# A sum made straight from PSUM behind a second transpose, and the normalisations of tokens moved from VectorE to GpSimd

## The reference

```python
x = x + _layernorm(_L0_attn_ref(_layernorm(x), ...))   # 16 heads of 64, latent width 64 for q and for k, v; rope; out + residual
x = x + _layernorm(_L0_ffn_ref(_layernorm(x), ...))    # router softmax, top 2 of 8 experts, hidden width 256, SiLU gate
```

## Time and profile before

| | us |
|---|---|
| median of 3 runs | 1662.54 (1661.48 to 1665.63) |
| the profiled execution, its own time | 1663.62 |
| its span | 1661.8 |
| PE busy (matmuls) | 1404.3, 85% |
| DVE busy | 1212.5, 73% |
| ACT busy | 1107.1, 67% |
| POOL busy | 1231.9, 74% |

### The profile page before, as it was taken

How to read it: one execution, slowest core, us unless ns; L and a number is a source line. 1 busy time by engine, 2 the same in 40 slices (tenths; PEclk the granted TensorE clock), 3 DMA queues, 4 the chain that set the end, 5 groups by cost and what they waited for, 6 DMA issues and landing times. The chain is left out here.

```text
span 1661.8 us, 45240 instructions
## 1 busy us (share of the span) xinstructions
PE 1404.3 (85%) x17718; PEld 904.0 (54%) x17718; DVE 1212.5 (73%) x2719; ACT 1107.1 (67%) x2136; POOL 1231.9 (74%) x749
## 2 busy tenths in 40 slices
PE   4899989998988989989988899999888887777630
PEld 1366656665545656656645556665455555566530
DVE  7788777777878788787777887777778875555353
ACT  2777767776667767767766677777666666355462
POOL 5588977986767678896766788987667788535574
PEclk7899999999999999999999999999999998789775
DMA  6333423422322223222321232322212421222332
GB/s 179 92 109 115 119 79 107 120 78 65 84 69 79 72 66 102 72 72 71 84 71 49 58 92 77 85 79 71 65 45 70 156 65 41 91 79 85 104 104 64
DMA packets 111232, 140.87 MB, mean 85 GB/s; under 512 B 17712, under 2 KB 59952, under 8 KB 110640
## 3 DMA queue, kind: packets, MB, share of 16 engines
q1 hardware_dynamic: 106928, 129.60, 27.9%
q0 software_dynamic: 4096, 8.40, 1.7%
HBM read 23.50 MB, written 19.92 MB: 26 GB/s over the span
## 5 line engine op out<-in xcount | busy, mean ns | idle before, releaser
L1844 POOL TENSOR_TENSOR probs_lo<-probs 128x1024 f16<-128x1024 f32 x312 | 655.8, 2109 | 233.2 <-ACT probs L1116 231.9
L1116 ACT ACTIVATE probs<-psum 128x512 f32<-128x512 f32 x1024 | 614.6, 602 | 228.3 <-PE psum L846 227.8
L1415 DVE CUSTOM_DVE_ANT_0 scan_out<-psum,ahead 128x512 f16<-128x512 f32 x512 | 349.0, 687 | 249.5 <-PE psum L744 223.8
L865 PE MATMUL psum<-cv,probs 128*128 128x66 f16 x4096 | 488.6, 195 | 23.7 <-POOL probs_lo L1844 23.7
L867 PE MATMUL psum<-cv,probs 128*128 128x64 f16 x4096 | 487.6, 196 | 0.0
L869 PE MATMUL psum<-cv,probs_lo 128*128 128x66 f16 x4096 | 486.2, 194 | 0.0
L867 PEld LDWEIGHTS psum<-cv,probs 128*128 128x128 bf16 x4096 | 388.1, 99 | 116.6 <-issue 13.2
L865 PEld LDWEIGHTS psum<-cv,probs 128*128 128x128 bf16 x4096 | 392.5, 99 | 87.5 <-POOL probs_lo L1844 20.4
L846 PE MATMUL psum<-q_max,k_ones 65*128 65x512 f16 x1024 | 401.8, 392 | 0.0
L844 PE MATMUL psum<-q_both,k_twice 128*128 128x512 f16 x1024 | 399.7, 390 | 0.0
L869 PEld LDWEIGHTS psum<-cv,probs_lo 128*128 128x128 f16 x4096 | 387.1, 100 | 0.0
(11 more groups left out here) (208 smaller groups left out, 1976.9 us busy)
## 6 DMA issues: line engine op xcount, KB each, us to landing
t_swapped<-t_sin SPq DMA_DIRECT2D x248, 128.0 KB, 2.1
k_twice<-qk_hi SPq DMA_DIRECT2D x128, 128.0 KB, 2.4
q_lone<-qk_hi SPq DMA_DIRECT2D x64, 128.0 KB, 2.4
q_both<-qk_hi SPq DMA_DIRECT2D x64, 128.0 KB, 2.3
q_both<-qk_lo SPq DMA_DIRECT2D x64, 128.0 KB, 2.4
q_max<-qk_hi SPq DMA_DIRECT2D x64, 128.0 KB, 2.4
k_ones<-qk_lo SPq DMA_DIRECT2D x64, 128.0 KB, 2.4
z_unit<-slots_in SPq DMA_DIRECT2D x46, 128.0 KB, 2.3
```

Source lines behind the costliest of these rows:

```text
L865: pe.matmul(acc, high[:, q * P:(q + 1) * P, 1], v[:, 0:VLO], start=opens, stop=False, skip_group_check=True)
L1116: act.activation(probs[s % 4][:, i, :], score_ps[tile % SCORE_BANKS], ACT.Exp, scale=SCALE).then_inc(probs_done, 1)
L1415: dve.tensor_tensor_reduce(scan_out[m % 2][:], bank[BANK_OF["base", n, m]], ahead[m % 2][:], 1.0, LOWEST, ALU.add, ALU.max, max_all[a][:, ...
L1844: pool.tensor_tensor(probs_lo[s % 4][:].rearrange("p a n -> p (a n)"), p, p.bitcast(BF16).rearrange("p (n two) -> p n two", two=2)[:, :, 1 ...
```

## The change

- `add_tokens` no longer reads `res_sb`. PE turns the same tokens of `oacc` a second time, in new jobs "again" at (2, 8) and (2, 10), and DVE makes `x_sb = x_sb * res_scale + psum`. That is the old sum times the token's deviation; `res_scale` is that deviation plus the inverse deviation of x. The four instructions for each half now read one operand from SBUF and one from PSUM.
- As the next norm does not see the token's scale but for its epsilon, its variance becomes `ln_var` (one more instruction on 128x8) with the bias `eps_twice`. `add_output` gives the scale back: four instructions of 128x128 for each half in place of one of 128x512.
- `normalise_batch` and `normalise_input` go to POOL. Each half is two instructions of 128x512, a subtraction and a multiplication with the token's numbers broadcast over the channels, at steps 3, 5, 7 and 9 of the pair, behind `rope_add`. For batch 3 all four stand together at unit 11, behind `low_hidden(11)`.
- Some statistics, means, deviations and inverses move by one step; ACT's two table changes go from step 15 to step 0 of the next pair.
- `route` compares the indices as they are, without the cast (line 1553).

```diff
-STAT0_AT, MEANS0_AT, DEV0_AT, INV0_AT = ((1, 12), (1, 13)), (1, 14), (1, 15), (2, 1)
-ADD_AT = ((2, 8), (2, 10))
-STAT1_AT, MEANS1_AT, DEV1_AT, INV1_AT = ((2, 12), (2, 13)), (2, 14), (2, 15), (3, 1)
-NORM_AT = ((3, 8), (3, 10))
+STAT0_AT, MEANS0_AT, DEV0_AT, INV0_AT = ((1, 12), (1, 14)), (1, 15), (2, 0), (2, 2)
+AGAIN_TURNS = ((2, 8), (2, 10))
+STAT1_AT, MEANS1_AT, DEV1_AT, INV1_AT = ((2, 12), (2, 14)), (2, 15), (3, 0), (3, 2)
+NORM_AT = ((3, 3), (3, 5), (3, 7), (3, 9))
...
-    return {("norm", 0): (k, 8), ("norm", 1): (k, 10), ("x", 0): (k, 11), ("x", 1): (k, 12),
+    return {("norm", 0): (k, 3), ("norm", 1): (k, 5), ("norm", 2): (k, 7), ("norm", 3): (k, 9), ("x", 0): (k, 11), ("x", 1): (k, 12),
...
+            if at == AGAIN_TURNS[half]:
+                jobs.append((1, ("again", epoch - 1, half)))
...
-PE_TOKENS, PE_INPUT, PE_LOGITS, PE_RANK = 3, 13, 15, 22
+PE_TOKENS, PE_AGAIN, PE_INPUT, PE_LOGITS, PE_RANK = 3, 7, 13, 15, 22
+POOL_NORM = 11
...
+                elif kind == "again":
+                    pe.wait_ge(x1_done, CHUNKS * n + (at + 1))
...
-                last.then_inc(mv_done[k], 1)
+                last.then_inc(mv_done[k] if k != 1 else mv1_parts, 1)
+                if k == 1:
+                    dve.wait_ge(mv1_parts, n + 1)
+                    dve.scalar_tensor_tensor(out=ln_var[:], in0=mv_of(0, n)[:, :, 1], scalar=LN_EPS, in1=mv_of(1, n)[:, :, 1],
+                                             op0=ALU.mult, op1=ALU.add).then_inc(mv_done[k], 1)
...
+            def residual_scale(n):
+
+                dve.wait_ge(dev_done[0], n + 1)
+                dve.tensor_tensor(res_scale[:], ln_dev[0][:], rstd_x[:, n * TILES:(n + 1) * TILES], ALU.add).then_inc(res_scaled, 1)
+
             def add_tokens(n, half):
-                dve.wait_ge(inv_done[0], n + 1)
+                dve.wait_ge(res_scaled, n + 1)
+                dve.wait_ge(o_turned, 2 * CHUNKS * n + CHUNKS + (half + 1))
+                src = job_bank("again", n, half)
                 for t in tile_range(half):
-                    last = dve.scalar_tensor_tensor(out=x_sb[:, t, :], in0=res_sb[:, t, :], scalar=inv_of(0, n)[:, t:t + 1],
-                                                    in1=x_sb[:, t, :], op0=ALU.mult, op1=ALU.add)
+                    last = dve.scalar_tensor_tensor(
+                        out=x_sb[:, t, :], in0=x_sb[:, t, :], scalar=res_scale[:, t:t + 1],
+                        in1=src[:, t % HALF_TILES * P:(t % HALF_TILES + 1) * P], op0=ALU.mult, op1=ALU.add)
                 last.then_inc(x1_done, 1)
-
-            def normalise_input(n, half):
-                dve.wait_ge(inv_done[1], n + 1)
-                for t in tile_range(half):
-                    last = dve.tensor_scalar(z_sb[:, t, :], x_sb[:, t, :], mv_of(1, n)[:, t, 0:1], inv_of(1, n)[:, t:t + 1],
-                                             ALU.subtract, ALU.mult)
-                last.then_inc(z_done, 1)
...
-                dve.tensor_tensor(x1_all[n][:, tiles, :], x1_all[n][:, tiles, :], y_got[n][:, 0, tiles, :], ALU.add).then_inc(result_done, 1)
+                for t in tile_range(half):
+                    last = dve.scalar_tensor_tensor(out=x1_all[n][:, t, :], in0=x1_all[n][:, t, :], scalar=inv_of(0, n)[:, t:t + 1],
+                                                    in1=y_got[n][:, 0, t, :], op0=ALU.mult, op1=ALU.add)
+                last.then_inc(result_done, 1)
...
+            def normalise_batch(b, half, part):
...
+                if part == 0:
+                    if b == 1:
+                        pool.wait_ge(ln_y_inverse, 4)
+                    else:
+                        pool.wait_ge(x_next, 16 * (b - 1))
+                    pool.tensor_tensor(rows, rows, over_rows(moments_x[:, at, 0]), ALU.subtract).then_inc(n_centred, 1)
+                else:
+                    pool.wait_ge(n_centred, CHUNKS * (b - 1) + (half + 1))
+                    pool.tensor_tensor(rows, rows, over_rows(rstd_y[:, at]), ALU.mult).then_inc(n_ready, 1)
+
+            def normalise_input(n, half, part):
...
+                if part == 0:
+                    pool.wait_ge(inv_done[1], n + 1)
+                    pool.tensor_tensor(rows, x_sb[:, tiles, :], over_rows(mv_of(1, n)[:, tiles, 0]), ALU.subtract).then_inc(z_centred, 1)
+                else:
+                    pool.wait_ge(z_centred, CHUNKS * n + (half + 1))
+                    pool.tensor_tensor(rows, rows, over_rows(inv_of(1, n)[:, tiles]), ALU.mult).then_inc(z_done, 1)
```

More of the change, by code:

```diff
@@ L1656, in beside @@
                     for half in range(CHUNKS):
-                        if (r, s) == when["norm", half]:
-                            normalise_batch(b, half)
                         if (r, s) == when["latent", half]:
@@ L1735, in beside_unit @@
                     inverses(1, EARLY)
-                    for half in range(CHUNKS):
-                        normalise_input(EARLY, half)
                 for part in ROUTE_PARTS:
@@ L1938, in _ @@
                 low_hidden(unit)
+                if unit == POOL_NORM:
+                    for half in range(CHUNKS):
+                        for part in range(2):
+                            normalise_input(EARLY, half, part)
                 if unit in SEND_UNITS:
```

66 lines of the change are left out of this document (40 added, 26 removed).

## The result

The changed kernel takes 1593.43 us (median of 4 runs, 1590.84 to 1596.16) against 1662.24 us (4 runs, 1661.48 to 1665.63) for the kernel before on the same chip. The ratio is 0.9582 [0.9561, 0.9604]: 68.8 us or 4.2% less. The profiled execution has a span of 1594.4 us and a mean TensorE clock of 0.947 (before 1661.8 and 0.927).

A forecast was written before the change was run, and what follows sets the result against it. It took PE as the bound, at 37.5 us per undisturbed pair, with nine pairs slowed by waits for DVE and a low clock. Terms -72 + 7 + 12 + 2 + 3 + 1.4 = -46.6 gave 1616 us, range 1597 to 1642.

The forecast's parts named there:

- term 6: Moving means, deviations and inverses by one step leaves the cost of ACT's table changes as it was: 0, up to 3 us either way.
- the cast: Removing the cast in `route` gains 0, as the pairs' waits stay with the comparisons behind it.
- the expert stage and the end: Unit 11's gain and loss cancel, transposes at unit 7 cost 1 us, the last half 0.4: +1.4 us.
- Term 3: The "again" jobs, PE turns and DVE adds in three pairs, cost 7 us, between 0 and 15.8.
- terms 4 and 7: POOL's added norm instructions in six pairs cost 12 us; z and x turns meeting POOL's later results cost 3 us.
- term 5: Six small DVE instructions with two SBUF operands, `residual_scale` and `ln_var`, may wait for POOL: 2 us, 0 to 12.
- terms 1 and 2: In the nine pairs, PE's waits for DVE (45.3 us) and the low clock behind them (27 us) go: together 72 us.
- costs nothing: Rival: POOL's added norm instructions fit in its 5.3 us of idle time per pair; 1601 us, chance 0.2.
- POOL takes DVE's place: Rival: POOL's work overruns PE's pace, six pairs keep their length, only the `add_tokens` pairs gain; 1647 us, chance 0.14.

The follow-up runs named there:

- Experiment 1: Kernel before with only the second transposes, the sum from PSUM and the token-scale work; norms, steps and cast as before: 1638.79 us, ratio 0.9846.
- experiment 2: Kernel before with only the norms moved to POOL as broadcast instructions: 1626.59 us, ratio 0.9797.
- Experiment 5: Changed kernel with each of the 24 broadcast norm instructions inside pairs done a second time on POOL into a spare tile: 1609.06 us, ratio 0.9692.
- experiment 6: Changed kernel with the norms back on DVE as rows of four 128x128 instructions, at steps 3 and 7: 1624.91 us, ratio 0.9789.
- experiment 10: Changed kernel with its broadcast norm instructions issued by DVE in place of POOL, at the same steps: 1648.17 us, ratio 0.9673.
- experiment 3: Kernel before with only the steps of statistics, means, deviations and inverses moved: 1658.46 us, ratio 0.9968.
- experiment 7: Changed kernel with statistics, means, deviations and inverses put back at their old steps: 1597.69 us, ratio 0.9619.
- Experiment 4: Kernel before with only the cast in the routing left out: 1659.1 us, ratio 0.998.
- experiment 12: The changed kernel repeated word for word on another chip, against the kernel before: 1592.07 us, ratio 0.9582.
- experiment 11: Changed kernel with only ranks, places and low rows moved to earlier steps of their pair: 1597.31 us, ratio 0.961.
- experiment 8: Changed kernel with only the norm of batch 3, at unit 11, back on DVE: 1594.29 us, ratio 0.9622.
- experiment 9: Changed kernel with routing, ranks, places and low rows moved to earlier steps of the same pairs: 1639.1 us, ratio 0.9629.

## Why the prediction was right in kind and low in size

**What bounds the kernel: right.** PE stood behind DVE in the nine pairs, and its clock was at 0.90 to 0.96 in them. With the stalls gone the nine pairs lost 58.1 us at equal cuts (48 predicted), and PEclk is 1.00 in eight of them.

**Which steps failed.** Two. First, the terms that were put at nothing or given the wrong sign: the moved steps (term 6) measured 5.3 us and the cast 3.3 by themselves, and the expert stage and the end took 4.4 us less and not 1.4 more. Second, the price of what was added in the nine pairs: terms 3, 4, 5 and 7 took back 24 us of the 72, some 10 too much. By their windows the sum from PSUM alone gained 21.4 us where my terms leave 17, and the norms alone 36.7 where they leave 31. Each is taken up below. Beside that, two readings of the rows were wrong.

**The removed waits and clock, terms 1 and 2 (-72): right within some 4 us.** Experiment 1 takes 21.4 us out of the three `add_tokens` pairs, where my sum for them was 26.2 - 7 - 2 = 17. The missing 4 us lie in these three terms together. The small instructions of term 5 or the "again" jobs cost less, or the removal was more; no run separates them. Term 3 itself can be read in the "tokens" pairs, which hold the same work: they take 118.3 us after, 5.9 over the three undisturbed pairs of the earlier trace rows, against 7 taken. Its upper end was wrong: of the 15.8 us that the earlier trace rows has over the earlier trace rows, 7.4 were the late cut.

**POOL's load, terms 4 and 7 (+15): too dear.** The waits and the clock of the six pairs were 46.1 us in my terms, and experiment 2 gained 36.7 there, so 9.4 were given back. Not all of that is POOL's: I had counted the waits for `max_turned` as gone whole, and 7.2 us of them are left in the six pairs after (1.2 in each). Whether POOL's load keeps them there isn't shown. Two more errors met. The form costs 1.04 us alone, not 1.27, but nearly 2 among DVE's work, which is outside the 1.2 to 1.4 that I expected; and I take it, from PE's short waits, that part of this was covered; no run shows it. Experiment 5 prices a further four at 2.9 us a pair, above my 2, which I put down to the last cover being gone. The rival "costs nothing" is refuted by it. The rival "POOL takes DVE's place" is refuted by experiment 2: the six pairs are 36.7 us shorter though POOL is busy 96% of them. DVE's `low` did get longer as expected, a mean of 1640 ns (before 1541 by the group of line 1436), and PE has no wait over 0.15 us for it in the nine pairs:

```profile
L1442 DVE TENSOR_TENSOR probs_lo<-probs 128x1024 f16<-128x1024 f32 x200 | 327.9, 1640 | 4.3 <-ACT probs L1129 4.0
```

**Why the norms were dear: only partly understood.** I took the meeting with POOL's long instructions at steps 8 and 10 as the cause, and wrote that each of the small instructions waits for one of POOL's. The timeline of DVE shows less than that. Before, one of the two rows of four in such a pair was held long and the other ran free (first two lines, here 1.10 us at step 8 and 6.43 at step 10). In experiment 6 both are held once (2.50 us), and in experiment 10 the single instructions take 1.2 to 1.6 us each (last two lines):

```profile
1216.47 1.10 DVE L1503 TENSOR_SCALAR res_sb<-x_sb,ln_mv,ln_inv 128x128 f32<-128x128 f32 x4
1221.63 6.43 DVE L1503 TENSOR_SCALAR res_sb<-x_sb,ln_mv,ln_inv 128x128 f32<-128x128 f32 x4
```
```profile
1165.87 2.50 DVE L1531 TENSOR_SCALAR res_sb<-x_sb,ln_mv,ln_inv 128x128 f32<-128x128 f32 x4
1178.01 2.50 DVE L1531 TENSOR_SCALAR res_sb<-x_sb,ln_mv,ln_inv 128x128 f32<-128x128 f32 x4
```
```profile
1163.56 1.23 DVE L1406 TENSOR_TENSOR res_sb<-x_sb,ln_mv 128x512 f32<-128x512 f32 x1
1168.34 1.56 DVE L1409 TENSOR_TENSOR res_sb<-res_sb,ln_inv 128x512 f32<-128x512 f32 x1
```

The two rows of experiment 6 hold DVE for 5.0 us of a pair, the four instructions of experiment 10 for 5.2 here; so it isn't their sum that makes the 21.4 us, but where and in how long pieces it falls. That a long piece holds back the scan behind it is shown by PE's waits for `max_turned` and `max_all`; how much is the length of a piece and how much its step is argued, not shown. The timeline of POOL after shows the same meeting from the other side; its norms take 1.9 to 2.0 us there, and PE's waits in that pair (shown above) hold none for POOL:

```profile
1148.36 1.91 POOL L1891 TENSOR_TENSOR res_sb<-x_sb,ln_mv 128x512 f32<-128x512 f32 x1 [0.99 <-DVE ln_inv L1497]
1150.23 1.89 POOL L1852 TENSOR_TENSOR probs_lo<-probs 128x1024 f16<-128x1024 f32 x1
1152.09 1.27 POOL L1836 TENSOR_TENSOR rot<-rot,t_swapped 128x512 f32<-128x512 f32 x1
1153.33 2.02 POOL L1894 TENSOR_TENSOR res_sb<-res_sb,ln_inv 128x512 f32<-128x512 f32 x1
```

By the Trainium skill, "SBUF — State Buffer", section Who interferes with whom, a VectorE instruction with two SBUF inputs or in a two-port mode and one of GpSimd that reads SBUF hold each other out of a shared port pair for whole instructions; these figures agree (1.04 us alone, 1.91 and 2.02 beside DVE). The Trainium skill's rule in "GPSIMD Engine Reference", section 4.1 Engine selection, that elementwise work belongs on VectorE, pointed the wrong way here: by experiments 6 and 10 both forms on DVE were slower than the broadcast one on POOL, by 29.0 and 7.6 us for six pairs. The prediction set 2.5 us of POOL, in two instructions, against 1.1 of DVE for its factor of two; the nearer pair of like instructions in its rows is 1.27 us and 0.69.

**The moved steps, term 6 (0, up to 3 either way): failed.** They gave 5.3 us alone (experiment 3) and cost 4.3 when undone (experiment 7). I had argued that a change of place costs nothing as the number of instructions is the same. But the pairs beside the table changes were not at PE's pace. At equal cuts the gain of experiment 3 lies in pairs 2 (4.2 us) and 3 (1.5), and in the changed kernel the steps are worth 6.7 us in pairs 1 to 3 (experiment 7). Whether the table change at step 0 or the statistics one step later does it was not tried apart and stays open.

**The cast (0): failed by a little.** Experiment 4 gave 3.3 us (0.3 to 6.1). I read that the waits stay with the comparisons; they do, and these became longer (the group of the comparison after, 1673 ns; in the kernel before 1071 and 680 for the two), but one instruction less stood in the queue:

```profile
L1565 DVE TENSOR_TENSOR hots<-ids_sb,top_at 128x64 f32<-128x64 f32 x4 | 6.7, 1673 | 0.0
```

**The expert stage and the end (+1.4): failed.** From the first SiLU to the end it took 223.3 us before, 218.8 after and again 218.8 in experiment 12, but 224.1 with the sum alone and 223.6 with the norms alone. So this gain of 4.5 us appears with both parts together only. On the other chips all kernels with the sum from PSUM and the norm of unit 11 on POOL take 218.5 to 221.1 us there (experiments 5, 7, 11 and 12), and with that norm on DVE 222.5 to 224.1 (experiments 1, 6 and 8); on the chip of experiments 9 and 10 it is 263.0 against 267.8. So most of it hangs on unit 11. Kernels with the same code in this stage differ by up to 2.6 us, so its size is rough. What links the two parts was not found.

**Sum of the miss, by the parts' medians.** Against what my terms gave for each: the sum from PSUM 25.6 for 16, the norms 33.7 for 31, the steps 5.3 for 0, the cast 3.3 for 0; that is 67.9 for 47. The zeros make 8.6 of the 21, the first part 9.6 (5.5 by its span). My range had its lower end at the case in which POOL's load is free; it held no gain for terms that I had set at nothing, so it was too short on that side. That 1593 lies near this end does not bear that case out: POOL's load has a price (experiment 5).

## What to carry to other kernels

When VectorE feeds the engine that bounds, look at how long it is taken at one step, and not only at how long it is busy: rows of small instructions, some of them held by a long one of GpSimd, cost 3.6 us more a pair than the same work in single broadcast instructions at separate steps, at nearly the same busy time (how much of it is the length of a piece and how much its step was not separated). An operand read from PSUM, even at the price of transposing it again on TensorE, took such a row from 6.60 to 1.12 us. And in a kernel whose pairs are not all at the pace of the bound, a moved or dropped instruction is not free in either direction: give it a term with both ends, as the zeros of this prediction show. And before two windows are compared, see that both are cut at the same place of the work: a cut at an instruction that the change itself moves shifts time from one window to the next, here 2.47 us each time.

## What the runs showed that I had not expected

On one chip the kernel before took 1703.08 us and not 1662. No trace of it on that chip is kept; the pairs of heads of experiment 9 took 1301.3 us there, as long as elsewhere. What follows the pairs took 278.8 us in experiment 9 and 234.8 in the changed kernel on the other chip. The group of the last gathers in experiment 9 has POOL idle for a store of rows:

```profile
L1904 POOL DMA_INDIRECT y_got<-slots_out,slot_of x64 | 60.8, 951 | 61.3 <-DMA slots_out<-y_sb 41.9
```

POOL's waits for that store are 41.9 us (two, the longest 36.2) where the changed kernel has one of 5.9: 36 us of the 44 between them. Experiment 10, on the same chip, has 42.7. Why that chip's store is late isn't known; it shows that kernels must be compared with runs of the kernel before on the same chip. The other surprise is how much one place gives to another: the pairs with `route` and with ranks and places differ by up to 6 us between kernels in which their own code is the same (125.2 and 131.4 us in the changed kernel, 131.9 and 126.4 with only the steps of pairs 1 to 3 put back).
